# VectorE's products of three batches moved among the last row turns, and tile 0's routing put first in the adapter layer

## The chip, the cores and the metric

The kernel runs on one core of one Trainium2 chip. The metric is device time in microseconds (us) of one execution. PE is TensorE, DVE is VectorE, ACT is ScalarE, POOL is GpSimd, and SP issues the DMAs.

## The reference, cut to what matters

Four residual blocks follow each other, each on a layer norm of x, which is 4 batches x 512 rows x 1024 columns. Only the first two are touched by the change.

```
def _L0_attn_ref(x):            # for each of the 1024 columns l: attention among the 4 batches
    q = transpose(x, (2, 0, 1))                       # l, n, c
    scores = einsum('lnc,lmc->lnm', q, q) / scale     # 4 x 4 for each l
    prob = softmax(scores)
    return x + transpose(einsum('lnm,lmc->lnc', prob, q), (1, 2, 0))

def _L0_ffn_ref(x, W_base, b_base, W_gate, A, B):
    result = x @ W_base.T + b_base
    probs = softmax(x @ W_gate.T)                     # 8 experts
    top_p, top_i = top_k(probs, 2); top_p /= sum(top_p)
    h = einsum('bnd,erd->bner', x, A) * route_w[..., None]
    return result + einsum('bner,eor->bno', h, B) * SCALING
```

Then come an attention with 32 heads and a second adapter layer, which the change leaves alone. One of the weights of that attention, the query weights, is prepared while the first adapter layer runs.

## The kernel before, in words

Every stage is one block of five written-out instruction streams, one for each engine, tied by semaphores. A stage begins when all engines have ended the stage before. The rows are 16 tiles of 128.

**First layer (`first`, L601 to L1015).** Each tile t is normed: `dve_stats` on DVE, `pool_rstd` on POOL, and then the normalisation itself on the engine that the string `Norm.ON` (L60) names for it, "d" for DVE and "a" for ACT. Even tiles go to DVE, odd ones to ACT. The a-tiles also need `pool_shift`. PE turns (transposes) the normed tile in two halves (L706) and ACT copies both out of PSUM into `hT` (L774), where a row is one of the 1024 columns and a batch is 512 elements long. `hT` has 8 parts j. For each j, DVE makes the six products of different batches (`product`, L818 to L824, one instruction of 512 elements and its accumulator), ACT the four squares (`square`, L749), DVE the softmax of the 4 x 4 scores (`softmax`, L826), and then the weighted sums are made by ACT (`weigh`), DVE (`weigh_more`, L857) and, through 128 x 256 diagonals that POOL writes (L921), by PE (`messages`, L685). DVE adds the messages to x (L863). Products and squares of j=0 and j=1 stand ahead of the loop over j. Those of j+2 are dealt out among the four row tiles c of the loop by `fourth(c)`, which cuts the list `pairs` in four. All products wait for all 16 tiles. In between, `side` runs the making of fused weights: `absorbed(G)` with loads of `wuk` and `wqn`, products on PE (L667), copies on ACT (L733) into four staging tiles `mst`, and stores. `fused(kt)` does the same for the output weights (L677, L741, L742). A load of `absorbed(2)` is issued by SP behind the stores of `absorbed(0)`. At the end of the stage the first 8 of 14 parts of the adapter layer's weights are split into a high and a low half-precision part by ACT (L1177) and DVE (L1184), and PE makes the first column chunk of tiles 0 and 1.

**Adapter layer (`lora_layer0`, L1187 to L1512).** PE follows the list `ORDER` (L1212): ("c", t, c) is column chunk c of tile t (24 matmuls), ("w", t) turns the routed factors of tile t (L1260), ("a", t) is the adapter's product (6 matmuls), ("s", n) is a small total. DVE makes the routing (`gate`, L1352 to L1382, 13 short instructions with one exponential on ACT, L1295), adds the chunks to x (`finish`, L1392) and then the adapter's part (`adapter`, L1400). POOL makes the low half of each normed tile (L176) and adds the bias to x (`add_bias`, L1453), for which `finish` waits. A tile t+2 is normed, split (ACT L171, POOL L176) and turned by a DMA (L183) while tile t is worked on.

For t=5 to 13 the query weights (`QueryWeights`) go along, one group g a tile: DVE weighs them (L402, L403), ACT squares them (L408), PE totals (L412), DVE and POOL make the scale (L416, L419), ACT writes the high part (`act_high`, L430) and DVE the low part (`dve_low`, L435). ACT's high part stands last in the turn of a tile. DVE's low part stands ahead of `finish`.

Of the kernel before, what the change touches and what calls it, by code (L numbers as in the profile page):

```python
# [56 lines left out]
class Norm:  # L57


    ON = "da" * 8 + "d" * 19 + "a" * 13 + "d" * 16  # L60
# [136 lines left out]
def layers(nc, a, out):  # L197
    root = ExitStack()
    with root:
# [34 lines left out]
        with ExitStack() as right:  # L234
            with ExitStack() as both:
                g["room"] = right.enter_context(nc.sbuf_tensor("N_room", [128, 6144], F, side="right"))
                g["s_c"] = root.enter_context(nc.semaphore("F0_c"))

                g["bk"] = bk = [banks.enter_context(nc.psum_tensor(f"bk{i}", [128, 512], F)) for i in range(2)]
                feed.place_first(g["room"])  # L240
# [12 lines left out]
            projections(**g)  # L253
# [346 lines left out]
def first(nc, a, wbd, mwd, cst, vec, half, ident, xb, norm, msq, lnr, room, feed, lw, ones, s_c, bk, keep, **_):  # L600
# [3 lines left out]
    hb = [room[:, 5120:6144]] + [ph.sb(f"h{i}", [128, D]) for i in range(1, 3)]  # L604
# [35 lines left out]
    pairs = [(n, m) for n in range(4) for m in range(n, 4)]  # L640
    apart = [p for p in pairs if p[0] != p[1]]

# [82 lines left out]
    def act(e):  # L725
        w = Waits(e)

        def absorbed(G):
            for k in range(2):
                n = staged("a", G, k)  # L730
                w.wait_ge(s_wp, 2 * G + k + 1)
                w.wait_ge(s_mst[n % 4], 16 * (n // 4))
                e.activation(mst[n % 4][:, :], wb[k][:, :], ACT.Copy).then_inc(s_we, 1)  # L733
# [34 lines left out]
        for t in range(NT):  # L768
            if t + 2 < NT and t % 2:
# [45 lines left out]
    def dve(e):  # L815
        w = Waits(e)

        def product(j, n, m):  # L818
            k = 6 * j + apart.index((n, m))
            w.wait_ge(s_hT, 2 * NT)  # L820
            w.wait_ge(s_tr, 2 * NT)
            w.wait_ge(s_sc, k)
            e.tensor_tensor_reduce(junk, hT[:, j, 512 * n:512 * n + 512], hT[:, j, 512 * m:512 * m + 512], 1.0, 0.0, ALU.mult, ALU.add,
                                   sc[:, j, n, m:m + 1]).then_inc(s_sc, 1)  # L824

        def softmax(j):  # L826
            w.wait_ge(s_sc, 6 * j + 6)
# [42 lines left out]
        for t in range(NT):  # L870
# [3 lines left out]
            if t + 2 < NT and t % 2 == 0:  # L874
                w.wait_ge(s_tr, 2 * t)
                norm.dve_apply(e, w, t + 2, hb[(t + 2) % 3][:, :], xb[:, t + 2, :])
        for n, m in apart:
            product(0, n, m)
# [3 lines left out]
        for n, m in apart:  # L882
            product(1, n, m)
# [27 lines left out]
    def pool(e):  # L911
# [15 lines left out]
        for t in range(NT):  # L927
            if t + 2 < NT and t % 2:
# [11 lines left out]
        feed.pool_low(e, w, 1)  # L940

    def sp(e):
# [54 lines left out]
        for j in range(KD):  # L997
# [3 lines left out]
            for c in range(4):  # L1001
                side(SIDE_J.get((j, c)))
        for n in range(4):
# [183 lines left out]
def lora_layer0(nc, a, cst, vec, half, ident, ones, xb, xd, s_xd, lnr, norm, feed, lw, wa, qw, ms, s_c, bk, **_):  # L1187
# [3 lines left out]
    W, BT, bias = lw.W, lw.BT, ph.sb("bias", [128, D])  # L1191
# [9 lines left out]
    s_xb, s_g, s_gx = ph.sem("xb"), ph.sem("g"), ph.sem("gx")  # L1201
# [10 lines left out]
    ORDER = [("c", 0, 1), ("c", 1, 1), ("w", 0), ("c", 0, 2), ("w", 1), ("a", 0), ("c", 1, 2), ("a", 1)]  # L1212
    for t in range(2, NT):
# [69 lines left out]
    def act(e):  # L1283
# [13 lines left out]
        for n in range(8, 10):  # L1297
            lw.act_split(e, w, n)
        feed.act_high(e, w, 2)
        gate_exp(0)  # L1300
        for n in range(10, 12):
            lw.act_split(e, w, n)
        gate_exp(1)
        high_w(0)
# [4 lines left out]
        for t in range(2, NT):  # L1309
            gate_exp(t)  # L1310
# [11 lines left out]
            if QW < t <= QW + 8:  # L1322
                qw.act_high(e, w, t - QW - 1)

    def dve(e):
# [75 lines left out]

        stats(2)
        lw.dve_split(e, w, 8)
        apply(2)
        lw.dve_split(e, w, 9)
        gate(0)
# [6 lines left out]
        low_w(1)  # L1413
        stats(3)
        apply(3)
        stats(4)
        finish(0)
# [3 lines left out]
        for t in range(2, NT):  # L1421
            stats(t + 3)
# [6 lines left out]
            gate(t)  # L1429
# [17 lines left out]
    def pool(e):  # L1447
        w = Waits(e)

        def add_bias(t):  # L1450
            norm.applied(w, N_F0 + t)
            w.wait_ge(lw.s_bias, 16)
# [12 lines left out]
        add_bias(0)  # L1465
        feed.pool_low(e, w, 2)
        add_bias(1)
# [20 lines left out]
    def sp(e):  # L1488
# [7 lines left out]
        e.dma_start(bias[:, :], a["b0"].partition_broadcast(128)).then_inc(lw.s_bias, 16)  # L1496
# [1032 lines left out]
```

## Time and profile before

| what | value |
|---|---|
| median of 3 runs | 1631.84 us (1630.63 to 1632.85) |
| the profiled execution | 1631.13 us, span 1629.3 us |
| PE busy | 1547.9 us, 95% |
| DVE busy | 1018.8 us, 63% |
| ACT busy | 868.9 us, 53% |
| POOL busy | 811.3 us, 50% |
| the first layer | 0 to about 171 us of the span |
| the adapter layer | about 171 to 404 us of the span |

Busy shares are means over all stages. The two stages that the change touches are the first quarter of the span, and each has its own limits. A row of the timeline gives start, duration, engine, line and tile, and in brackets how long the engine stood idle before it and what released it. A row with "x2" merges two instructions.

### The profile page before, as it was taken

The page shows a single profiled execution, that of the slowest core. Times are in us where ns is not written, and L with a number is a line of the kernel's source. Part 1 is how long each engine was busy: PE and PEld are TensorE (multiplying, and loading weights), DVE is VectorE, ACT ScalarE, POOL GpSimd, SP SyncE. Part 2 cuts the span into 40 slices and gives each one's busy share as a digit, 9 for nine tenths or more (in the row PEclk, how much of TensorE's full clock was granted, in tenths as well). Part 3 has the DMA queues.
Part 4 walks back from the last instruction along what each step waited for, and adds up shares of the span by engine and source line. Part 5 has one row for each costly group of instructions (what it writes and reads, how often), then busy time and mean ns, then how long its engine had stood idle before and what let it go on. Part 6 is the DMA issues. An engine that isn't in the chain of part 4 may idle for free. (4 is left out here: it accounts for less than half of the span.)

```text
span 1629.3 us, 31927 instructions
## 1 busy us (share of the span) xinstructions
PE 1547.9 (95%) x12366; PEld 950.2 (58%) x12366; DVE 1018.8 (63%) x2747; ACT 868.9 (53%) x1654; POOL 811.3 (50%) x699
## 2 busy tenths in 40 slices
PE   5898899999989999999999999889999999999998
PEld 4655455555556776777777777644444444465554
DVE  7898857776778888888888888832110010344433
ACT  6886222221759999999999999931210000211110
POOL 4223244444957888888888888830010000244440
PEclk9999899999999999999999999999999999999999
DMA  9894334444756999999998999997763331233331
GB/s 359 297 330 149 91 88 107 143 142 128 154 120 112 187 173 189 179 184 187 195 190 174 184 185 173 178 208 226 176 167 80 101 91 26 75 66 84 83 86 65
DMA packets 560263, 249.82 MB, mean 153 GB/s; under 512 B 502256, under 2 KB 535152, under 8 KB 559984
## 3 DMA queue, kind: packets, MB, share of 16 engines
q1 hardware_dynamic: 560112, 247.78, 66.1%
q8 instruction: 98, 1.61, 0.4%
q14 instruction: 53, 0.43, 0.1%
HBM read 73.68 MB, written 48.23 MB: 75 GB/s over the span
## 5 line engine op out<-in xcount | busy, mean ns | idle before, releaser
L1967 POOL TENSOR_TENSOR xb<-xb 128x1280 f16<-128x1280 f32 x128 | 335.6, 2622 | 7.8 <-ACT xb L1870 7.8
L1862 ACT ACTIVATE xb<-bk,D_sv,qw_c 128x512 f32<-128x512 f32 (+3 forms) x512 | 289.3, 623 | 4.4 <-DVE D_sv L1925 4.2
L1916 DVE TENSOR_REDUCE bk<-bk 128x1 f32<-128x512 f32 (+3 forms) x512 | 228.3, 492 | 20.5 <-PE bk L1812 19.9
L92 POOL TENSOR_SCALAR mv<-mv 128x1 f32<-128x1 f32 x64 | 31.2, 488 | 279.1 <-DVE mv L87 278.1
L1870 ACT ACTIVATE xb<-xb 128x1280 f16<-128x1280 f32 x128 | 162.7, 1271 | 13.1 <-DMA xb<-xb 9.3
L1803 PE MATMUL bk<-kTh,D_QTh 128*128 128x512 f16 (+3 forms) x512 | 153.4, 300 | 6.3 <-ACT xb L1862 6.2
L1804 PE MATMUL bk<-kTl,D_QTh 128*128 128x512 f16 (+3 forms) x512 | 153.2, 299 | 0.0
L1805 PE MATMUL bk<-kTh,D_QTl 128*128 128x512 f16 (+3 forms) x512 | 146.5, 299 | 0.0
L1827 PE MATMUL D_t<-vh,xb 128*128 128x65 f16 x1280 | 131.5, 194 | 4.7 <-DMA xb<-xb 3.0
L1828 PE MATMUL D_t<-vl,xb 128*128 128x65 f16 x1280 | 131.6, 193 | 0.0
L1829 PE MATMUL D_t<-vh,xb 128*128 128x65 f16 x1280 | 131.0, 193 | 0.0
L1827 PEld LDWEIGHTS D_t<-vh,xb 128*128 128x128 f16 x1280 | 119.1, 97 | 5.3 <-DMA xb<-xb 3.2
L2086 DVE SCALAR_TENSOR_TENSOR xb<-bk,ms_c,xb 128x512 f32<-128x512 f32 x22 | 15.5, 747 | 167.0 <-PE bk L50 167.0
L1828 PEld LDWEIGHTS D_t<-vl,xb 128*128 128x128 f16 x1280 | 118.9, 98 | 0.4
L1829 PEld LDWEIGHTS D_t<-vh,xb 128*128 128x128 f16 x1280 | 119.1, 97 | 0.0
L1940 DVE TENSOR_TENSOR D_QTl<-D_t,D_QTh 128x512 f16<-128x512 f32 x128 | 88.6, 692 | 46.9 <-ACT D_QTh L1879 46.9
L2408 POOL TENSOR_TENSOR xb<-xb,F_bias 128x1024 f32<-128x1024 f32 x16 | 38.2, 2393 | 131.7 <-DMA F_mean<-in_cst 131.7
L1973 POOL TENSOR_TENSOR D_os<-D_on,D_os 128x256 f16<-128x256 f32 x128 | 87.5, 684 | 10.7 <-ACT D_os L1886 10.7
L527 POOL TENSOR_TENSOR D_qs<-D_qs,keep 128x256 f32<-128x256 f32 x84 | 61.0, 727 | 58.6 <-DVE keep L522 58.6
L171 ACT ACTIVATE N_hl<-N_h 128x1024 f16<-128x1024 f32 x26 | 27.4, 1054 | 107.4 <-DVE N_h L105 107.2
L50 PE MATMUL bk<-E_mh,ow_ot 128*128 128x512 f16 x220 | 83.4, 379 | 0.0
L48 PE MATMUL bk<-E_mh,ow_ot 128*128 128x512 f16 x220 | 83.4, 379 | 0.0
(331 smaller groups left out, 4383.9 us busy)
## 6 DMA issues: line engine op xcount, KB each, us to landing
od<-D_os SPq DMA_DIRECT2D x32, 512.0 KB, 4.5
xd<-xb SPq DMA_DIRECT2D x16, 512.0 KB, 4.2
ow_raw<-mwd SPq DMA_DIRECT2D x16, 512.0 KB, 4.7
xb<-xd SPq DMA_DIRECT2D x16, 512.0 KB, 5.9
out_x<-xb SPq DMA_DIRECT2D x16, 512.0 KB, 3.0
xb<-in_x SPq DMA_DIRECT2D x6, 1024.0 KB, 13.6
A_wo<-in_wo SPq DMA_DIRECT2D x6, 1024.0 KB, 7.5
ow_raw<-in_w SPq DMA_DIRECT2D x16, 384.0 KB, 4.3
```

Source lines behind the costliest of these rows:

```text
L1803: e.matmul(ps, qh, kT[0][:, k0:k0 + M], start=i > 0, stop=False)
L1804: e.matmul(ps, qh, kT[1][:, k0:k0 + M], start=False, stop=False)
L1805: e.matmul(ps, ql, kT[0][:, k0:k0 + M], start=False, stop=False)
L1827: e.matmul(o, pt[:, c, :], v[0][:, t, 0:65], start=j == 0, stop=False)
L1828: e.matmul(o, pt[:, c, :], v[1][:, t, 0:65], start=False, stop=False)
L1829: m = e.matmul(o, pt[:, 10 + c, :], v[0][:, t, 0:65], start=False, stop=j == i)
L1862: m = e.activation(p[:, AT[i]:AT[i] + N], Sb[n % 4][:, c:c + N], ACT.Exp, scale=qw.col(qw.NEG, g), bias=s[:, 7 - i:8 - i])
L1870: e.activation(P2[u % 3][:, 0:1280], P[u % 3][:, :], ACT.Copy).then_inc(s_ph, 1)
L1916: m = e.tensor_reduce(minima(u, i), Sb[n % 4][:, c:c + N], AX.X, ALU.min)
L1940: e.tensor_tensor(lo[:, :], t_bank("t", u)[:, :], hi[:, :], ALU.subtract).then_inc(s_tl, 1)
L1967: e.tensor_tensor(P2[u % 3][:, 1280:2560], P[u % 3][:, :], P2[u % 3][:, 0:1280], ALU.subtract).then_inc(s_pl, 1)
L1973: e.tensor_tensor(o[:, :, 1, 64 * h:64 * h + 64], on[u % 2][:, :, :], o[:, :, 0, 64 * h:64 * h + 64], ALU.subtract).then_inc(s_ol, 1)
```

## The change

Four edits stand in the diff.

1. First layer: tiles 14 and 15 are both normed by DVE. The six products of j=0 and j=1 that need only batches 0 to 2 wait for tiles 0 to 11 alone and run directly behind DVE's last norm. Their unused elementwise output goes to the staging tile `mst[3]`, so ACT's first use of it waits for them. The list `pairs` is in another order, so the third quarter of a loop has one product and the last has two.
2. The bias of the adapter layer gets its place in the first layer (it takes over the buffer of `hb[1]`), is loaded near the stage's end, and POOL adds it to tiles 0 and 1 in the first layer, not in the adapter layer.
3. Adapter layer: DVE begins with the routing of tile 0. The order of the parts, norms, `finish` and routing of tiles 0 to 2 is another on DVE and ACT, and PE's `ORDER` has the chunks of tile 2 between the adapters of tiles 0 and 1.
4. For t=6 to 13 ACT makes the query weights' high part first in its turn, not last.

```
-    ON = "da" * 8 + "d" * 19 + "a" * 13 + "d" * 16
+    ON = "da" * 7 + "d" * 21 + "a" * 13 + "d" * 16
...
-    hb = [room[:, 5120:6144]] + [ph.sb(f"h{i}", [128, D]) for i in range(1, 3)]
+    hb = [room[:, 5120:6144], bias, ph.sb("h2", [128, D])]
...
-    pairs = [(n, m) for n in range(4) for m in range(n, 4)]
+    pairs = [(n, m) for m in range(4) for n in range(m + 1)]
+    TIMES = [(j, p) for j in range(2) for p in apart[:3]] + [(j, p) for j in range(2) for p in apart[3:]]
+    TIMES += [(j, p) for j in range(2, KD) for p in apart]
...   act, absorbed
+                w.wait_ge(s_sc, 6 if n == 3 else 0)
...   dve, product
-            w.wait_ge(s_hT, 2 * NT)
-            w.wait_ge(s_tr, 2 * NT)
+            w.wait_ge(s_hT, 8 * m + 8)
...
+            if k >= 6:
+                w.wait_ge(s_tr, 2 * NT)
...   dve, after the last norm
-        for n, m in apart:
+        for j in range(2):
+            for n, m in apart[:3]:
+                product(j, n, m)
+        for n, m in apart[3:]:
             product(0, n, m)
         softmax(0)
...
-        for n, m in apart:
+        for n, m in apart[3:]:
             product(1, n, m)
...   pool, end of the first layer
+        for t in range(2):
+            norm.applied(w, N_F0 + t)
+            w.wait_ge(lw.s_bias, 16)
+            e.tensor_tensor(xb[:, row(t), :], xb[:, row(t), :], bias[:, :], ALU.add).then_inc(s_xb, 1)
...   sp, first layer, ahead of the turns
+        w.wait_ge(s_msg, 28)
+        e.dma_start(bias[:, :], a["b0"].partition_broadcast(128)).then_inc(lw.s_bias, 16)
...   adapter layer
-    ORDER = [("c", 0, 1), ("c", 1, 1), ("w", 0), ("c", 0, 2), ("w", 1), ("a", 0), ("c", 1, 2), ("a", 1)]
-    for t in range(2, NT):
+    ORDER = [("c", 0, 1), ("c", 1, 1), ("w", 0), ("c", 0, 2), ("w", 1), ("c", 1, 2), ("a", 0), ("c", 2, 0), ("a", 1), ("c", 2, 1),
+             ("w", 2), ("c", 2, 2), ("a", 2)]
+    for t in range(3, NT):
...   act
-        for n in range(8, 10):
+        lw.act_split(e, w, 8)
+        gate_exp(0)
+        for n in range(9, 12):
             lw.act_split(e, w, n)
         feed.act_high(e, w, 2)
-        gate_exp(0)
-        for n in range(10, 12):
-            lw.act_split(e, w, n)
+        high_w(0)
         gate_exp(1)
-        high_w(0)
...
         for t in range(2, NT):
+            if QW < t <= QW + 8:
+                qw.act_high(e, w, t - QW - 1)
             gate_exp(t)
...
-            if QW < t <= QW + 8:
-                qw.act_high(e, w, t - QW - 1)
...   dve
+        gate(0)
+        lw.dve_split(e, w, 8)
         stats(2)
-        lw.dve_split(e, w, 8)
+        lw.dve_split(e, w, 9)
         apply(2)
-        lw.dve_split(e, w, 9)
-        gate(0)
...
         low_w(1)
+        finish(0)
         stats(3)
         apply(3)
-        stats(4)
-        finish(0)
         adapter(0)
         finish(1)
         adapter(1)
         for t in range(2, NT):
+            if t == 2:
+                gate(t)
+                stats(t + 2)
             stats(t + 3)
             apply(t + 2)
...   pool, adapter layer
-        add_bias(0)
         feed.pool_low(e, w, 2)
-        add_bias(1)
```

## Rows read from the trace of the kernel before

**Rows 1.** Windows, one stretch: busy time (instructions) of PE, PEld, DVE, ACT, POOL, clock, DMA.
```profile
130.00:140.00 10.00, 8.46 (x40) 5.53 (x38) 9.21 (x25) 8.26 (x21) 2.09 (x3) 1.00 0.57 199
```

**Rows 2.** Timeline of all engines, the last row turns.
```profile
35.38 1.24 ACT L110 ACTIVATE N_room<-xb,mv 128x1024 f32<-128x1024 f32 x1 [0.33 <-POOL mv L100]
36.52 1.06 ACT L774 ACTIVATE F_room<-A_tr 128x512 f32<-128x512 f32 x2
...
39.57 0.69 DVE L823 CUSTOM_DVE_ANT_0 N_room<-F_room 128x512 f32<-128x512 f32 x1 [5.30 <-ACT F_room L774]
```

**Rows 3.** The same timeline, from the first store to the loop over j.
```profile
41.55 0.88 SPq L962 DMA_DIRECT2D wbd<-keep  x2
...
43.98 0.29 DVE L830 COPY A_sc<-A_sc 128x3 f32<-128x3 f32 x3
...
48.79 3.67 PE L667 MATMUL bk<-N_room 128*128 128x128 f32 x16 [3.23 <-DMA N_room<-in_wqn]
...
56.06 0.29 DVE L830 COPY A_sc<-A_sc 128x3 f32<-128x3 f32 x3 [0.17 <-ACT N_room L754]
...
61.13 1.41 DVE L857 SCALAR_TENSOR_TENSOR A_h<-F_room,A_ex,A_h 128x512 f32<-128x512 f32 x2 [2.07 <-ACT A_h L765]
```

**Rows 4.** Timeline, end of the first layer and start of the next.
```profile
158.55 4.79 DVE L1184 SCALAR_TENSOR_TENSOR F_room<-F_room,F_sc 128x784 f16<-128x784 f32 x3
159.81 2.70 POOL L176 TENSOR_TENSOR N_room<-N_room 128x1024 f16<-128x1024 f32 x1 [2.02 <-ACT N_room L171]
...
164.34 3.81 DVE L1184 SCALAR_TENSOR_TENSOR F_room<-F_room,F_sc 128x768 f16<-128x768 f32 x4 [0.67 <-ACT F_room L1177]
...
171.49 0.32 PE L48 MATMUL bk<-F_room,N_room 128*128 128x384 f16 x1 [0.48 <-PEq L1008]
```

**Rows 5.** Timeline, routing of tile 0.
```profile
176.84 2.36 POOL L1453 TENSOR_TENSOR xb<-xb,F_bias 128x1024 f32<-128x1024 f32 x1 [2.35 <-DMA F_bias<-in_b]
176.91 2.31 DVE L1365 CAST F_sm<-F_mi 128x2 f32<-128x2 uint32 x1
184.38 0.47 PE L1260 MATMUL F_tr<-cst,F_hw 128*128 128x128 f32 x1 [4.93 <-DVE F_hw L1381]
```

**Rows 6.** Timeline, tile 1's adapter, tile 2's routing, PE's turns of tiles 2 and 3.
```profile
198.46 0.39 PE L48 MATMUL F_tr<-F_room,F_hwh 128*128 128x512 f16 x1 [2.21 <-DVE xb L1400]
205.63 0.23 DVE L1358 TENSOR_SCALAR F_sm<-bk,F_sc 128x8 f32<-128x8 f32 x1 [1.56 <-PE bk L50]
207.84 0.29 DVE L1381 TENSOR_TENSOR F_hw<-bk,F_sm 128x128 f32<-128x128 f32 x1
209.33 0.27 PE L1260 MATMUL F_tr<-cst,F_hw 128*128 128x128 f32 x1
222.51 0.27 PE L1260 MATMUL F_tr<-cst,F_hw 128*128 128x128 f32 x1
```

**Rows 7.** Windows, the stretch behind tile 1's adapter.
```profile
198.50:202.50 4.00, 4.00 (x13) 1.70 (x14) 3.96 (x8) 0.00 (x0) 0.41 (x1) 0.57 0.71 131
```

**Rows 8.** Groups of DVE by form, 171 to 223 us: busy us, mean ns, idle before.
```profile
L1400 DVE SCALAR_TENSOR_TENSOR xb<-F_tr,F_sc,xb 128x512 f32<-128x512 f32 x6 | 4.2, 747 | 0.2
L83 DVE BATCH_NORM_STATS2 st<-xb 128x6 f32<-128x512 f32 x5 | 3.4, 687 | 3.2 <-PEq L1008 3.2
L1392 DVE SCALAR_TENSOR_TENSOR xb<-F_o,F_sc,xb 128x384 f32<-128x384 f32 x4 | 2.4, 612 | 0.4 <-PE F_o L50 0.4
```

**Rows 9.** Timeline, one step with query weights (t=10) and the next exponential.
```profile
325.18 2.35 POOL L1453 TENSOR_TENSOR xb<-xb,F_bias 128x1024 f32<-128x1024 f32 x1
327.44 1.28 DVE L435 SCALAR_TENSOR_TENSOR F_room<-F_room,qw_c 128x1024 f16<-128x1024 f32 x1 [1.52 <-ACT F_room L430]
331.01 0.38 PE L412 MATMUL F_tr<-qw_c,ones 128*128 128x1 f32 x2 [0.80 <-DVE xb L1400]
336.22 0.20 ACT L1295 ACTIVATE F_sm<-F_sm 128x1 f32<-128x1 f32 x1 [8.82 <-DVE F_sm L1363]
```

**Rows 10.** Waits, 240 to 372 us: who for whom, us in total, times, longest.
```profile
PE F_tr L412 <- DVE xb L1400: 8.6, 8, 1.6
```

More of the change, by code:

```diff
@@ L239, in layers @@
                 g["bk"] = bk = [banks.enter_context(nc.psum_tensor(f"bk{i}", [128, 512], F)) for i in range(2)]
+                g["bias"] = both.enter_context(nc.sbuf_tensor("F0_bias", [128, D], F))
+                g["s_xb"] = root.enter_context(nc.semaphore("F0_xb"))
                 feed.place_first(g["room"])
@@ L597, in pe_turned, with first @@
             w.wait_ge(self.s_o[j % 3], 16 * self.G * (1 if j % 3 else 2) + 16 * (j // 3))
-def first(nc, a, wbd, mwd, cst, vec, half, ident, xb, norm, msq, lnr, room, feed, lw, ones, s_c, bk, keep, **_):
+def first(nc, a, wbd, mwd, cst, vec, half, ident, xb, norm, msq, lnr, room, feed, lw, ones, s_c, bk, keep, bias, s_xb, **_):
     ph = Scope(nc, "A")
     hT = lw.room[:, :].rearrange("p (k n) -> p k n", k=KD)
-    hb = [room[:, 5120:6144]] + [ph.sb(f"h{i}", [128, D]) for i in range(1, 3)]
+    hb = [room[:, 5120:6144], bias, ph.sb("h2", [128, D])]
     tr = [ph.bank(f"tr{i}") for i in range(2)]
@@ L768, in act @@
         for t in range(NT):
-            if t + 2 < NT and t % 2:
+            if t + 2 < NT and norm.ON[t + 2] == "a":
                 w.wait_ge(s_tr, 2 * t)
@@ L818, in product @@
         def product(j, n, m):
-            k = 6 * j + apart.index((n, m))
-            w.wait_ge(s_hT, 2 * NT)
-            w.wait_ge(s_tr, 2 * NT)
+            k = TIMES.index((j, (n, m)))
+            w.wait_ge(s_hT, 8 * m + 8)
             w.wait_ge(s_sc, k)
-            e.tensor_tensor_reduce(junk, hT[:, j, 512 * n:512 * n + 512], hT[:, j, 512 * m:512 * m + 512], 1.0, 0.0, ALU.mult, ALU.add,
+            if k >= 6:
+                w.wait_ge(s_tr, 2 * NT)
+            e.tensor_tensor_reduce(junk if k >= 6 else mst[3][:, :], hT[:, j, 512 * n:512 * n + 512], hT[:, j, 512 * m:512 * m + 512], 1.0, 0.0, ALU.mult, ALU.add,
                                    sc[:, j, n, m:m + 1]).then_inc(s_sc, 1)
         def softmax(j):
-            w.wait_ge(s_sc, 6 * j + 6)
+            w.wait_ge(s_sc, 6 * j + 6 if j else 9)
             w.wait_ge(s_sq, 4 * j + 4)
@@ L873, in dve @@
                 norm.dve_stats(e, w, t + 3, xb[:, t + 3, :])
-            if t + 2 < NT and t % 2 == 0:
+            if t + 2 < NT and norm.ON[t + 2] == "d":
                 w.wait_ge(s_tr, 2 * t)
                 norm.dve_apply(e, w, t + 2, hb[(t + 2) % 3][:, :], xb[:, t + 2, :])
-        for n, m in apart:
+        for j in range(2):
+            for n, m in apart[:3]:
+                product(j, n, m)
+        for n, m in apart[3:]:
             product(0, n, m)
@@ L927, in pool @@
         for t in range(NT):
-            if t + 2 < NT and t % 2:
+            if t + 2 < NT and norm.ON[t + 2] == "a":
                 norm.pool_shift(e, w, t + 2)
@@ L1184, in dve_split, with lora_layer0 @@
         e.scalar_tensor_tensor(lo, self.source(self.again + n), self.scale(c), hi, ALU.mult, ALU.subtract).then_inc(self.s_wl, 1)
-def lora_layer0(nc, a, cst, vec, half, ident, ones, xb, xd, s_xd, lnr, norm, feed, lw, wa, qw, ms, s_c, bk, **_):
+def lora_layer0(nc, a, cst, vec, half, ident, ones, xb, xd, s_xd, lnr, norm, feed, lw, wa, qw, ms, s_c, bk, bias, s_xb, **_):
     ph = Scope(nc, "F0")
     qw.place(*[lw.room[:, o:o + 2048] for o in lw.free])
-    W, BT, bias = lw.W, lw.BT, ph.sb("bias", [128, D])
+    W, BT = lw.W, lw.BT
     junk = lw.room[:, lw.free[1] + 2048:lw.free[1] + 2560].bitcast(H16)
@@ L1200, in lora_layer0 @@
     s_tp, s_hi, s_tr = ph.sem("tp"), ph.sem("hi"), ph.sem("tr")
-    s_xb, s_g, s_gx = ph.sem("xb"), ph.sem("g"), ph.sem("gx")
+    s_g, s_gx = ph.sem("g"), ph.sem("gx")
     s_fin = ph.sem("fin")
@@ L1428, in dve @@
                 qw.dve_weigh(e, w, t - QW, vec, lnr, wa)
-            gate(t)
+            if t > 2:
+                gate(t)
             if t == NT - 1:
@@ L1451, in add_bias @@
             norm.applied(w, N_F0 + t)
-            w.wait_ge(lw.s_bias, 16)
             e.tensor_tensor(xb[:, row(t), :], xb[:, row(t), :], bias[:, :], ALU.add).then_inc(s_xb, 1)
@@ L1494, in store @@
             e.dma_start(xd[row(t), :, :], xb[:, row(t), :]).then_inc(s_xd, 16)
-        e.dma_start(bias[:, :], a["b0"].partition_broadcast(128)).then_inc(lw.s_bias, 16)
         wa.sp_load(e)
```

## The prediction

> **What bounds the kernel now.** I read the two stages of the change in five views. The windows [rows 1] say that in the loop over j of the first layer DVE is busy 9.21 of 10 us and PE 8.46: DVE sets the pace there, and a shift of its start is handed on. The timeline of the last row turns [rows 2] shows DVE idle for 5.30 us until 39.57, behind ACT: ACT norms tile 15 at 35.38 and then copies out three tiles one after the other, from 36.52 until it releases DVE at 39.57, about 1.0 a tile. ACT ends last there. The next view [rows 3] shows what follows. The stores of `absorbed(0)` leave at 41.55, the load behind them lets PE go at 48.79 after 3.23 us of waiting, ACT's squares of j=1 end just ahead of DVE's softmax at 56.06 (0.17 idle), and DVE waits 2.07 for ACT's first weighing of j=1 at 61.13. So the start of the loop hangs on ACT and on that load, not on DVE's products.
>
> In the adapter layer PE waits 4.93 us at 184.38 for the routing of tile 0 [rows 5], 2.21 us at 198.46 for tile 1's adapter [rows 6], and 8.6 us in eight totals of the query weights [rows 10]. The profiled execution took 1631.13 us for a span of 1629.3, 0.71 under the median, so a difference in the span is taken off the median.
>
> **Step 1, the last row turns.** Tile 15's norm leaves ACT. DVE can start it when the scale is there, about 35.1 (ACT's needs the shift besides, 0.3 more), and has it done at 35.9; PE turns the tile from about 36.0. ACT goes on with tile 13's copies at 34.95 instead of 36.52 (tile 12's pair ends then), and three tiles at the pace of before end at 37.95 instead of 39.53. Gain: 1.58 us in `hT` complete.
>
> The six early products take 0.73 each (0.69 and a step), 4.4 us, from 35.9 to 40.3. Three more of j=0 then end at 42.45. Without early products, six would begin at 37.98 and end at 42.4. So for softmax(0), now at 43.98 [rows 3], the early products buy nothing; it comes at 42.5 either way. For softmax(1) they take three products (2.2 us) off DVE ahead of 56.06. Before, DVE and ACT came out together there, and both move up 1.5, so DVE's extra 2.2 become idle time behind ACT. I cost them at 0, with up to 0.2 either way. ACT's new wait for six products (due 40.3) lies before the copy that has it (about 42.3).
>
> ACT, the stores at 41.55 and the load all move by 1.58, and the loop over j with them. Its DVE work is the same. The new order of pairs lets PE's transposes at c=0 start a product (0.7) earlier, but DVE's pace rules, so 0. Step 1: 1.6 us gained. Its lower end is 0, if the load does not come earlier; its upper 2.0.
>
> **Step 2, the bias on POOL in the first layer.** Before, two bias additions (2.36 each [rows 5]) and a low half ran on POOL beside tile 0's routing. Its CAST of two elements began at 176.91 and ended at 179.22, with POOL's addition (176.84 to 179.20). DVE stood still until POOL was through, and from there to PE's turn at 184.38 two more POOL instructions passed. The same shows at 158.55 [rows 4]: three splits took 4.79 in place of 2.9 while one POOL instruction ran from 159.81 to 162.51. An instruction of one engine waits for the other's end.
>
> The Trainium skill says this too (SBUF — State Buffer, section "Who interferes with whom"): DVE with two SBUF inputs or in a two-port mode and a GpSimd instruction exclude each other for a whole instruction, and the one that issues first wins. The rows above agree. What the rule speaks against is step 4.
>
> Now the additions follow POOL's low half of tile 1 at 162.5. They collide with DVE's five last splits, about 0.95 each [rows 4, 8]. In turns: the third split to 163.3, addition to 165.7, split 4 to 166.65, addition to 169.0, three splits to 171.9. Before, DVE ended at 168.15 and PE at 171.01, with the next stage's PE at 171.49 [rows 4]. So DVE now ends last and the stage ends 0.9 later. Bounds: 0 (if POOL's additions slip in between) and 2. The bias's load took under 5.6 us (stage start to 176.84 [rows 4, 5]) and is issued, behind the 28th message, some 15 us ahead of the additions. Cost: 0.9 us.
>
> **Step 3, order of tiles 0 to 2.** I write the new order down from the stage's start S. Durations: routing 2.5 (205.63 to 208.13), statistics 1.45, norm 0.75, split 0.95, `finish` 1.55, adapter 1.35 (its two instructions overlap) [rows 6, 8]. For PE, 13.18 a tile [rows 6] less 0.25 for the turn and 1.3 for six adapter matmuls gives 3.9 a chunk.
> - DVE: routing(0) to 2.7, split 8, statistics 2, split 9 to 6.1, norm 2 to 7.6, splits 10 and 11 to 9.5. Then routing(1) meets POOL's low half of tile 2 (9.5 to 11.65) and ends at 13.2.
> - PE: two chunks to 8.0, turn 0 at once (it waited 4.93), chunk (0,2) to 12.1, then 1.2 of waiting for routing(1), chunk (1,2) to 17.5, adapter 0, chunk (2,0) to 22.7, adapter 1, chunk (2,1), turn 2 at 28.0, chunk (2,2) to 32.1.
> - DVE meanwhile: `finish(0)` to 16.6, tile 3 to 19.75, adapter 0 to 21.1, `finish(1)`, adapter 1 to 24.9, routing(2) to 27.4, statistics 4 and 5 to 30.3, norm 4 to 31.05. ACT's high half comes first, so the low part of tile 2's factors is there at 32.8 and PE waits 0.7. POOL's low half and bias end at 36.7, `finish(2)` and adapter 2 at 39.65, tile 5's norm at 41.85, routing(3) at 44.35.
> - PE is through with (3,0) and (3,1) at 41.95 and waits 2.5. Turn 3 at 44.4.
>
> Before, turn 3 stood at 222.51, which is 51.2 behind the stage's start of about 171.3 [rows 4, 6]. So 6.8 are gained up to there. The adapter's `finish(3)` is then late behind the bias, and the totals after tile 3 lose 1.0 more. A wait of 2.21 was followed by a stretch at a granted clock of 0.57 [rows 7], mostly the lower level of 1.2 GHz, worth some 2 us of PE. The new wait of 2.5 may bring the same; as DVE is the later one there, I take half, 1.0. Step 3: 6.8 - 1.0 - 1.0 = 4.8 gained, with bounds 1 and 7.
>
> **Step 4, the query weights' high part first.** In one step [rows 9] DVE waits 1.52 for ACT's L430, makes the low part at 327.44 and `finish` behind it, and PE's total waits 0.80. With the high part made ahead of the routing's exponential, DVE could start 1.5 earlier, at 325.95. Taken alone, adapter t would be bound by PE from then on: 0.55 less of PE's wait of 0.80 in the steps like this one (four of them), about twice that in the three with longer waits (up to 1.6 [rows 10]), some 5.4 us in all. But POOL's bias addition runs from 325.18 to 327.53, and the low part has two SBUF inputs, like the splits that stood still at 158.55. It would then begin at 327.5, as now, and `finish` also waits for the addition. I take 0.1 a step, 0.3 to 0.5 in all. By the skill's rule just named it is 0 and by shared bandwidth some 3.
>
> **Sum.** 1.6 - 0.9 + 4.8 + 0.4 = 5.9 us. 1631.84 - 5.9 = 1625.9; I say 1626.
>
> **Rivals.**
> - A: step 4 pays in full, since the low part is not held up, and 5.4 come in place of 0.4: 1621. For it: eight waits that all name DVE [rows 10]. Against it: rows 4 and 5.
> - B: step 1 is lost, since the load sets PE's 48.79 and does not move: 1627.5. For it: PE did wait for that DMA. Against it: the load is issued behind the stores that wait for ACT, and PE's wait counts from that issue.
> - C: the new order of tiles 0 to 3 only puts the wait off. Two statistics stand ahead of norm 4, so bias 2, `finish(2)`, routing(3) stay late for two or three tiles, each with a spell at the lower clock. Step 3 is then worth 1 to 2: 1629.3.
> - D, slower: ACT's high part at the head of its turn waits for POOL's scale and holds up the exponential and the high half of tile t+2, so PE's turn waits. Now the exponential comes at 336.22, 5.2 behind the total at 331.01, after ACT has been idle for 8.82 [rows 9]; total and scale take about 1.3 of the 5.2. From a delay of over 4 us on, each of eight steps costs the excess, and with 2 us each it is 16 less the 6: 1642. It decides where the totals come late, which they don't in this trace.
> - E: the first edit doesn't bring the norm of tile 15 forward, because DVE's turn needs ACT's copies of the ring anyway; this is B's time again and held within it.
>
> **Chances.** Forecast 0.48, A 0.15, B with E 0.13, C 0.19, D 0.03, and 0.02 for something else. Faster by over 0.2% (below 1628.6, about what a measurement of this kernel can tell from no change): nearly all of the forecast, A and B, a third of C: 0.77. Within 0.2%: 0.18. Slower: 0.05. The range reaches from A's 1621 to a little above C: 1620.5 to 1630.
>
> **What would show it.** Step 1: ACT's last copy (L774) ends near 38 and DVE's loop starts near 59.6 instead of 61.13; the early products stand from 35.9. Step 2: POOL's two L1453 in the first layer, DVE's last split of the stage after PE's last chunk. Step 3: no wait at turn 0, a wait of 2 to 3 us at turn 3. Step 4: L435 starts on the end of POOL's addition, its duration over 2 us in place of 1.28, and PE's waits at L412 stay near 8 us. If L412's waits fall to 3 us, step 4 was judged wrong; if turn 3 waits 5 us or more, C.

## The result and the profile after

The kernel after takes 1622.44 us (median of 6 runs, 1620.99 to 1623.14), the kernel before 1631.78 us in the runs beside it (6 runs, 1630.33 to 1632.85). The ratio is 0.9941, with a 95% interval of 0.9931 to 0.9951: 9.3 us faster, where 5.9 were forecast. The time lies inside the range given, but 1622.44 is nearer to rival A's 1621 than to the forecast of 1626, so the number alone doesn't say which account was right. The traces do. The profiled execution took 1622.44 us for a span of 1620.7, so its span is 8.6 shorter than the span before.

The places that the prediction followed, in the two profiled executions (us from the start of the span; the forecast is the prediction's sum up to that place):

| place | before | after | moved | forecast |
|---|---|---|---|---|
| DVE's norm of tile 14 (no part of the change) | 33.49 | 32.36 | -1.1 | 0 |
| `hT` complete, ACT's first square | 39.56 | 36.87 | -2.7 | -1.6 |
| DVE's start of the loop over j | 61.13 | 57.77 | -3.4 | -1.6 |
| adapter layer, PE's first chunk | 171.49 | 168.60 | -2.9 | -0.7 |
| PE's turn of tile 3 | 222.51 | 212.29 | -10.2 | -7.5 |
| PE's turn of tile 4 | 237.27 | 227.64 | -9.6 | -5.5 |
| PE's first matmul of the next stage | 404.88 | 394.20 | -10.7 | -5.9 |
| end of the span | 1629.3 | 1620.7 | -8.6 | -5.9 |

The first line comes from the load of tile 1's x. DVE's statistics of that tile wait for it, and start at 6.12 in this execution against 7.43 before; of that, 1.1 us are left at tile 14's norm. In the traces of all kernels here this start lies anywhere between 6.12 and 8.00, so it is taken off before the first layer is read. At the other end, 2.1 of the 10.7 us were lost again behind the adapter layer, in code that is the same. The other kernels below ended between 0.9 us to the good (the one with the bias alone, 5.4 ahead at 399.45 and 6.3 at the end) and 1.4 to the bad there. So this is probably the one execution's and not the change's, which no run settles. It is why the parts are measured below inside their own stage.

First layer, timeline of the kernel after. Columns as in the rows ahead of the prediction: start us, duration us, engine, line, operation, tiles, shapes, and in brackets the idle time before it and who ended it.
```profile
33.95 0.81 DVE L105 TENSOR_SCALAR N_room<-xb,mv 128x1024 f32<-128x1024 f32 x1 [0.82 <-POOL mv L95]
34.68 0.68 DVE L831 CUSTOM_DVE_ANT_0 A_mst<-F_room 128x512 f32<-128x512 f32 x1
...
35.70 1.14 ACT L781 ACTIVATE F_room<-A_tr 128x512 f32<-128x512 f32 x2
36.87 0.63 ACT L761 ACTIVATE N_room<-F_room 128x512 f32<-128x512 f32 x1
...
38.86 0.88 SPq L977 DMA_DIRECT2D wbd<-keep  x2
...
46.06 3.04 PE L673 MATMUL bk<-N_room 128*128 128x128 f32 x16 [3.19 <-DMA N_room<-in_wqn]
...
52.71 0.29 DVE L838 COPY A_sc<-A_sc 128x3 f32<-128x3 f32 x3 [1.52 <-ACT N_room L761]
...
57.77 1.41 DVE L865 SCALAR_TENSOR_TENSOR A_h<-F_room,A_ex,A_h 128x512 f32<-128x512 f32 x2 [1.53 <-ACT A_h L772]
```
The norm of tile 15 now stands on DVE, the products directly behind it, and ACT's last copy ends at 36.8. Everything that hung on ACT in [rows 2, 3] has moved with it: the first store by 2.69, PE's wait for the load by 2.73 (its length is the same, 3.23 and 3.19). Most of what the early products saved turned into idle time: DVE waits 1.52 for ACT ahead of its second softmax, where it waited 0.17 [rows 3].

End of the first layer and routing of tiles 0 and 1, same kernel and view:
```profile
156.16 2.70 POOL L176 TENSOR_TENSOR N_room<-N_room 128x1024 f16<-128x1024 f32 x1 [2.02 <-ACT N_room L171]
158.82 6.10 POOL L955 TENSOR_TENSOR xb<-xb,F_bias 128x1024 f32<-128x1024 f32 x2
...
160.69 6.90 DVE L1201 SCALAR_TENSOR_TENSOR F_room<-F_room,F_sc 128x768 f16<-128x768 f32 x4 [0.67 <-ACT F_room L1194]
...
168.60 0.32 PE L48 MATMUL bk<-F_room,N_room 128*128 128x384 f16 x1 [0.48 <-PEq L1025]
...
176.40 0.27 PE L1278 MATMUL F_tr<-cst,F_hw 128*128 128x128 f32 x1
...
178.24 1.47 DVE L1380 TENSOR_TENSOR F_sm<-F_sm 128x1 f32<-128x1 f32 x1
...
181.50 0.33 PE L1278 MATMUL F_tr<-cst,F_hw 128*128 128x128 f32 x1 [0.94 <-DVE F_hw L1398]
```
The two additions and the last four splits wait for each other: 6.10 us for what takes 4.7, and 6.90 in place of the 3.81 of [rows 4]. In return there is no wait at PE's turn of tile 0, which was 4.93 [rows 5].

The turn of tile 2 and what follows, same kernel and view:
```profile
202.35 2.35 POOL L1472 TENSOR_TENSOR xb<-xb,F_bias 128x1024 f32<-128x1024 f32 x1
204.73 1.01 DVE L1409 SCALAR_TENSOR_TENSOR xb<-bk,F_sc,xb 128x256 f32<-128x256 f32 x2 [4.06 <-POOL xb L1472]
...
212.29 0.33 PE L1278 MATMUL F_tr<-cst,F_hw 128*128 128x128 f32 x1 [2.22 <-DVE F_hw L1398]
...
218.62 1.05 PE L328 MATMUL F_tr<-wa_c,ones 128*128 128x1 f32 x8 [0.80 <-DVE xb L1417]
```
The wait was put off: `finish(2)` stands 4.06 us for POOL's addition, and PE 2.22 at tile 3's turn, behind it. No drop of the clock followed this time (windows of the kernel after, columns as in [rows 1]):
```profile
212.50:216.50 4.00, 4.00 (x26) 2.41 (x25) 0.55 (x2) 0.28 (x1) 3.71 (x2) 1.00 0.70 70
```
In four us 26 matmuls ran at a granted clock of 1.00, where [rows 7] had 13 at 0.57.

One step with query weights (t=9, as t=10 in [rows 9]), timeline, then the waits of PE from 228 to 362 us:
```profile
307.61 1.15 ACT L433 ACTIVATE F_room<-F_room,qw_c 128x1024 f16<-128x1024 f32 x1 [5.85 <-POOL qw_c L422]
...
314.40 0.27 PE L1278 MATMUL F_tr<-cst,F_hw 128*128 128x128 f32 x1
...
314.82 2.35 POOL L1472 TENSOR_TENSOR xb<-xb,F_bias 128x1024 f32<-128x1024 f32 x1
...
315.48 2.77 DVE L438 SCALAR_TENSOR_TENSOR F_room<-F_room,qw_c 128x1024 f16<-128x1024 f32 x1
```
```profile
PE F_tr L415 <- DVE xb L1417: 7.5, 8, 1.3
```
ACT's high part is there nearly 7 us early and DVE starts its low part without waiting for it, but the low part lasts 2.77 in place of 1.28 and ends at 318.2, 1.1 behind the end of POOL's addition (317.2).

### The profile page after: what moved, and what is told of

Its sections match the earlier page's. It is cut to its first block and busy times, and to the rows that moved or that the text cites. A ratio compares the mean times of both kernels' runs of the same rounds, so it can differ in the third digit from the quotient of the medians.

```text
span 1620.7 us, 31929 instructions
## 1 busy us (share of the span) xinstructions
PE 1546.0 (95%) x12366; PEld 949.4 (59%) x12366; DVE 1028.4 (63%) x2748; ACT 868.4 (54%) x1653; POOL 813.1 (50%) x698
## 5 line engine op out<-in xcount | busy, mean ns | idle before, releaser
L48 PE MATMUL bk<-E_mh,ow_ot 128*128 128x512 f16 x220 | 83.4, 379 | 0.0
L49 PE MATMUL bk<-E_ml,ow_ot 128*128 128x512 f16 x220 | 83.4, 379 | 0.0
```

What stands on the lines that cost most here:

```text
L48: e.matmul(out, a[0], b[0], start=start, stop=False, **kw)
L49: e.matmul(out, a[0], b[1], start=False, stop=False, **kw)
```

## The experiments

Each time is a median of 5 to 12 executions. Each ratio, with its 95% interval, is to the kernel before on the same chip, whose medians there were 1631.4 to 1631.6 us. The kernels were timed in four groups on four chips: the first four; then e_bias, e_order, b_ahead and b_both; then m_old, b_old and b_lean; then e_later. Across groups the ratios compare better than the medians.

**The bare first edit, e_norm15.** Kernel before, with tile 15's norm moved to DVE:
```
-    ON = "da" * 8 + "d" * 19 + "a" * 13 + "d" * 16
+    ON = "da" * 7 + "d" * 21 + "a" * 13 + "d" * 16
-            if t + 2 < NT and t % 2:
+            if t + 2 < NT and norm.ON[t + 2] == "a":
```


> The kernel before with tile 15 normed by VectorE and nothing else changed. If the gain of the first layer comes from taking that norm off ScalarE: hT is complete 1.6 us sooner (VectorE's first product near 38.0 by the span of before, against 39.57), the loop over j starts about 2 us sooner, and the time falls by 1.5 to 2.5 us. If the early products are what pays: no more than 0.5 us.

Measured: 1629.91 us, ratio 0.9993 (0.9984 to 1.0002). The time alone can't tell it from nothing. Its trace can. From the norm of tile 14 to `hT` complete it was 6.07 us before and is 4.51 here (33.93 to 38.44), 1.56 less against 1.58 forecast. From that norm to the loop over j it was 27.64 and is 25.94, 1.7 less.

**The early products alone, e_products.** The new order of pairs, the six early products and ACT's wait for them, without the norm:
```
+        for j in range(2):
+            for n, m in apart[:3]:
+                product(j, n, m)
+        for n, m in apart[3:]:
             product(0, n, m)
...
```


> The kernel before with the six early products and the new order of pairs; tile 15 stays with ScalarE. If the products buy nothing by themselves: hT complete as before, the softmax of j=0 about 2.2 us sooner (three products less behind it), but the squares of j=0 and j=1 on ScalarE and the load behind the first stores keep their places, so VectorE only waits longer for ScalarE, and the time moves by less than 0.5 us. If VectorE's products set the start of the loop: 1.5 to 2 us less time.

Measured: 1631.3 us, ratio 1.0 (0.9991 to 1.0009). DVE's timeline of this kernel:
```profile
56.95 0.29 DVE L834 COPY A_sc<-A_sc 128x3 f32<-128x3 f32 x3 [2.96 <-ACT N_room L757]
```
DVE has 2.2 us of products less to do here and waits 2.96 for ACT instead of 0.17. ACT's squares set this point, as the prediction had it. One part of the expectation missed: `hT` is complete 6.58 us behind tile 14's norm, not 6.07. The early products run on DVE from 34.45, beside POOL's two short instructions for the scale and shift of tile 15. These take 0.86 and 0.46 there instead of 0.56 and 0.26, and ACT's norm of the tile waits for them. With the norm on DVE ahead of the products (e_first, the kernel after) this doesn't occur.

**The whole first edit, e_first.** Both together.

> The kernel before with the whole first edit (tile 15's norm and the early products) and nothing else. If the two only add up as the steps say: as with tile 15's norm alone, within 0.5 us of it, 1.5 to 2.5 us under the kernel before. If the pair is worth more than its parts, since the products would otherwise end behind ScalarE's squares once the norm has moved: at least 1 us under the run with the norm alone.

Measured: 1629.08 us, ratio 0.9986 (0.9977 to 0.9995), a gain of 0.8 to 3.8 us. From tile 14's norm to the loop it is 26.26 us, 0.3 more than with the norm alone. In this execution the 16 matmuls behind the load took 3.78 us at a granted clock of 0.50, against 2.69 at 0.73 with the norm alone; that alone is more than the 0.3. So the two traces don't show that the products are worth nothing. With the norm alone, DVE's six products of j=1 run without a pause until 54.7, ACT's squares are done at 53.9, and ACT then waits 1.67 for DVE where it waits 0.84 here. In that execution the early products would have saved up to 0.8 us.

**The fourth edit alone, e_high.** Kernel before, ACT's high part ahead of the exponential:
```
         for t in range(2, NT):
+            if QW < t <= QW + 8:
+                qw.act_high(e, w, t - QW - 1)
             gate_exp(t)
```


> The kernel before with ScalarE's high part of the query weights first in its turn, and nothing else. If VectorE's low part then waits for POOL's bias addition (one excludes the other): L435 takes about 2.8 us in place of 1.28 and ends where the addition ends plus 1.1, TensorE's eight waits at L412 fall from 8.6 to between 7 and 8 us in all, and the time falls by 0.5 to 1.2 us. If the two engines share the port by parts: L435 takes under 2 us, the waits fall to 3 to 5 us and the time falls by 3 to 5 us.

Measured: 1630.6 us, ratio 0.9996 (0.9987 to 1.0006). Its timeline and its waits, 228 to 362 us:
```profile
325.64 2.78 DVE L435 SCALAR_TENSOR_TENSOR F_room<-F_room,qw_c 128x1024 f16<-128x1024 f32 x1
...
330.71 0.38 PE L412 MATMUL F_tr<-qw_c,ones 128*128 128x1 f32 x2 [0.69 <-DVE xb L1400]
```
```profile
PE F_tr L412 <- DVE xb L1400: 7.6, 8, 1.3
```
The totals' waits fall from 8.6 [rows 10] to 7.6, and this agrees with the kernel after (7.5). The low part is held up by POOL's addition here too; rival A is out.

**The bias alone, e_bias.** Kernel before with the second edit: the bias row loaded in the first layer and POOL's additions for tiles 0 and 1 made there. The order of tiles 0 to 2 is the old one.
```
         feed.pool_low(e, w, 1)
+        for t in range(2):
+            norm.applied(w, N_F0 + t)
+            w.wait_ge(lw.s_bias, 16)
+            e.tensor_tensor(xb[:, row(t), :], xb[:, row(t), :], bias[:, :], ALU.add).then_inc(s_xb, 1)
...
-        add_bias(0)
         feed.pool_low(e, w, 2)
-        add_bias(1)
```


> The kernel before with only the bias moved: loaded and added to tiles 0 and 1 by POOL at the end of the first layer. The additions exclude VectorE's splits there, so the stage ends 0.8 us later; in the adapter layer the routing of tile 0 no longer meets them, only POOL's low half of tile 2. If those additions were what held the routing of tile 0: TensorE's wait of 4.93 us at the turn of tile 0 falls to about 1, and the time falls by 2 to 3.5 us net. If VectorE's order (statistics, splits and norm ahead of the routing) was the cause: the wait stays above 3 us and the time is within 1 us of before.

Measured: 1623.95 us, ratio 0.9957 (0.9943 to 0.9971), 7.6 us faster. The first timeline is of this kernel; PE's first chunk in it is at 172.84.
```profile
181.79 0.33 PE L1268 MATMUL F_tr<-cst,F_hw 128*128 128x128 f32 x1 [0.99 <-DVE F_hw L1389]
...
187.67 0.38 PE L48 MATMUL F_tr<-F_room,F_hwh 128*128 128x512 f16 x1 [1.28 <-DVE F_room L1192]
...
194.71 0.39 PE L48 MATMUL F_tr<-F_room,F_hwh 128*128 128x512 f16 x1 [1.68 <-DVE xb L1408]
...
217.09 0.27 PE L1268 MATMUL F_tr<-cst,F_hw 128*128 128x128 f32 x1
```
The wait at tile 0's turn falls from 4.93 to 0.99 with DVE's old order. Tile 3's turn comes 44.25 us behind the first chunk and tile 4's 59.0, against 65.78 before and 59.04 in the kernel after. So this edit alone gives the whole gain of the adapter layer's first four tiles.

The gain is more than twice the 2 to 3.5 us that I had expected, and the clock is the reason. Windows from the first chunk to tile 4's turn, and of four us behind tile 0's turn; first the kernel before, then this one:
```profile
171.49:237.27 65.78, 58.33 (x327) 33.17 (x328) 47.05 (x124) 15.12 (x28) 27.20 (x23) 0.92 0.32 81
184.38:188.38 4.00, 4.00 (x13) 2.01 (x14) 3.67 (x15) 1.50 (x4) 0.00 (x0) 0.50 0.18 33
```
```profile
172.84:231.84 59.00, 54.74 (x327) 31.84 (x327) 42.74 (x124) 15.13 (x28) 22.58 (x21) 1.00 0.33 81
181.79:185.79 4.00, 4.00 (x25) 2.40 (x25) 3.67 (x15) 1.58 (x5) 0.00 (x0) 1.00 0.56 102
```
Of the 6.8 us, 3.2 are shorter waits (7.41 in all before, 4.22 here). The other 3.6 are PE's own time: the same 327 matmuls take 58.33 us at a mean clock of 0.92 before, and 54.74 at 1.00 here. Before, the clock fell behind both long waits, 4.93 and 2.21. Here the waits are 0.99, 1.28 and 1.68, and it never fell.

**Bias and order, e_order.** The same with the third edit (the new `ORDER`, routing ahead of statistics, `finish(0)` before tile 3).

> The kernel before with the bias moved and the new order of tiles 0 to 2 (edits 2 and 3). By the written-out order: turn of tile 0 without a wait, a wait of 2.2 to 2.5 us at the turn of tile 3, and that turn 43.8 to 44.4 us behind the stage's start in place of 51.2; the time falls by 5.5 to 7 us less what the later stages take back, so 4.5 to 6. If most of this comes from moving the bias alone, it lies within 1.5 us of the run with only the bias moved.

Measured: 1625.17 us, ratio 0.9966 (0.9952 to 0.9979). The order adds nothing on top of the bias: tile 3's turn is 43.70 behind the first chunk (0.5 earlier than with the bias alone), tile 4's 60.19. The 1.2 us by which this is later than in the kernel after are the clock: it fell behind a wait of 2.22, and behind the same wait in the kernel after it didn't (timeline, then windows of this kernel):
```profile
215.97 0.33 PE L1269 MATMUL F_tr<-cst,F_hw 128*128 128x128 f32 x1 [2.22 <-DVE F_hw L1389]
```
```profile
216.00:220.00 4.00, 4.00 (x15) 2.06 (x16) 0.37 (x2) 0.28 (x1) 3.88 (x2) 0.57 0.33 62
```

**All but the order, m_old.** The kernel after without the third edit:
```
-    ORDER = [..., ("c", 1, 2), ("a", 0), ("c", 2, 0), ("a", 1), ("c", 2, 1), ("w", 2), ("c", 2, 2), ("a", 2)]
+    ORDER = [("c", 0, 1), ("c", 1, 1), ("w", 0), ("c", 0, 2), ("w", 1), ("a", 0), ("c", 1, 2), ("a", 1)]
-        gate(0)
+        stats(2)
         lw.dve_split(e, w, 8)
-        stats(2)
+        apply(2)
         lw.dve_split(e, w, 9)
-        apply(2)
+        gate(0)
...
```


> Edits 1, 2 and 4 with the old order of tiles 0 to 2 (the kernel after without edit 3). Theory (taking POOL's two additions out of the stage's head is what pays, the order adds nothing): 1621.2 us, between 1620.2 and 1622.6, so ratio about 0.9935 to the kernel before and a little under the kernel after; no wait of PE at turn 0 over 1.1 us, turn 4 about 59 us behind the stage's first instruction, as in the run with the bias alone. Rival (the order is worth the 4.8 us that the prediction gave it): 1627 us, turn 4 at 64.

Measured: 1621.87 us, ratio 0.9943 (0.9929 to 0.9956). That is the kernel after's 0.9941, and tile 4's turn is 59.00 behind the first chunk, again as in it. The third edit is worth nothing that can be told in the kernel after, neither for nor against.

**The additions moved within the stage, e_later.** Kernel before, one edit:
```
-        add_bias(0)
         feed.pool_low(e, w, 2)
-        add_bias(1)
         norm.pool_rstd(e, w, N_F0 + 3)
         feed.pool_low(e, w, 3)
+        add_bias(0)
+        add_bias(1)
```


> The kernel before with POOL's additions of the bias row for tiles 0 and 1 put behind its low parts of tiles 2 and 3, instead of ahead of them; nothing else changed. Theory (the additions cost their time where they meet VectorE's splits and routing of the stage's first 10 us): PE's wait at turn 0 falls from 4.93 us to about 1, as in the run with the bias moved to the first layer; the additions (2.36 us each) would then start near 23 us behind the stage's first instruction, where that run has VectorE's finish(0) some 19.5 us behind it, so finish(0) waits 4 to 5 us for them, and of the 7.6 us some 3 are left: 1628.5 us, 1627 to 1630. Rival (the additions cost what they take wherever they are in this stage): 1631.5 us, nothing gained. Rival (their waits are hidden there, moving them within the stage is as good as moving them out): 1624 us.

Measured: 1631.65 us, ratio 1.0005 (0.9997 to 1.0014). The time is that of the first rival, the mechanism that of the theory. The timeline of this kernel (its first chunk at 171.93):
```profile
180.89 0.33 PE L1260 MATMUL F_tr<-cst,F_hw 128*128 128x128 f32 x1 [1.00 <-DVE F_hw L1381]
...
193.37 4.64 POOL L1453 TENSOR_TENSOR xb<-xb,F_bias 128x1024 f32<-128x1024 f32 x2
195.74 1.01 DVE L1392 SCALAR_TENSOR_TENSOR xb<-bk,F_sc,xb 128x256 f32<-128x256 f32 x2 [4.18 <-POOL xb L1453]
...
198.12 0.61 PE L48 MATMUL F_tr<-F_room,F_hwh 128*128 128x512 f16 x1 [6.00 <-DVE xb L1400]
```
The wait at tile 0's turn fell to 1.00, as expected, so the additions beside the routing were what caused it. But `finish(0)` then waited 4.18 for them and PE 6.00 at tile 1's adapter, where it was 2.21 [rows 6]. My expectation left 3 us of gain, and all of it was paid back. Out of the stage, the same additions cost 0.8 us.

**One tile ahead, b_ahead.** The kernel after, with POOL making tile t+1's addition where it made tile t's:
```
+        add_bias(2)
         norm.pool_rstd(e, w, N_F0 + 4)
...
-                add_bias(t)
+                add_bias(t + 1)
```


> The changed kernel with POOL adding each tile's bias one tile ahead (tile 2's behind the low half of tile 3, tile t+1's behind the low half of tile t+2), so that no finish waits for it. The wait of 4.06 us of VectorE ahead of finish of tile 2 goes, and with it TensorE's 2.2 us at the turn of tile 3: 2 to 3 us less time. The low part of the query weights still meets a POOL addition of the same length at the same place, so if exclusion is what holds TensorE's totals, their waits stay at 0.68 to 1.33 each. If it was the wait for the bias that held them, they fall to 0.3 and the time falls by 5 us or more.

Measured: 1618.26 us, ratio 0.9926 (0.9913 to 0.994). The median is 4.2 below that of the kernel after, which was timed in another group. By the ratios (0.9941 there) it is 2.4, and the two intervals overlap a little. Timeline:
```profile
202.19 1.00 DVE L1409 SCALAR_TENSOR_TENSOR xb<-bk,F_sc,xb 128x256 f32<-128x256 f32 x2
...
203.95 2.35 POOL L1472 TENSOR_TENSOR xb<-xb,F_bias 128x1024 f32<-128x1024 f32 x1
```
`finish(2)` no longer waits, PE doesn't wait at tile 3's turn (211.51, 41.33 behind its first chunk at 170.18), and tile 4's turn is 56.09 behind it instead of 59.04.

**The same on the old order, b_old.** m_old with that addition ahead.

> The same with POOL's addition of the bias row one tile ahead of PE from tile 2 on. Theory (the 4 us that this gave on top of the kernel after came from POOL's order at every tile, whatever the order of tiles 0 to 2): 1617.2 us, between 1616 and 1618.5, under the 1618.3 that it gave with the new order. Rival (it only took back the waits that the new order of tile 2 had made, 4.06 us of VectorE ahead of finish(2) and 2.22 us of PE at turn 3, which the old order has not): the same as the run without it, 1621 us.

Measured: 1623.06 us, ratio 0.9946 (0.9933 to 0.996). No gain over m_old, and tile 4's turn stays 59.00 behind the first chunk: the rival was right. The addition ahead takes away a wait that only the new order has. Together the two give 2.9 us in the trace. On top of the moved bias, neither gives anything by itself.

**Without the early products, b_lean.** b_old without them.

> The same without the early products and the new order of pairs; tile 15's norm stays on VectorE. Theory (tile 15's norm on VectorE is all that pays in the first layer; in the profiled runs the diagonal blocks' loop started 25.94 us behind tile 14's norm with it alone, 26.26 with the products too): same as with them, within 0.5 us. Rival (the early products give what the prediction's range allowed them above zero, or the 0.8 us by which the medians of these two kernels alone differed): 0.8 us slower.

Measured: 1621.12 us, ratio 0.9939 (0.9926 to 0.9953), beside 0.9946 (0.9933 to 0.996) with them. The early products are worth nothing that these runs can tell; the intervals would hide the 0.8 us of e_norm15's trace.

**The low part late, b_both.** b_ahead, with DVE's weighing (L405, L406) behind the routing and the low part behind the total:
```
             if t > 2:
                 gate(t)
+            if QW <= t < QW + 8:
+                qw.dve_weigh(e, w, t - QW, vec, lnr, wa)
...
-                qw.dve_low(e, w, t - QW - 1)
...
+            if QW < t <= QW + 8:
+                qw.dve_low(e, w, t - QW - 1)
```


> As the run before it, and VectorE's low part of the query weights moved behind the adapter and the total of its tile, the weighing behind the routing. Now nothing long stands between the low part of the routed factors and finish. If exclusion by POOL's addition was what kept the eight waits at the totals: they fall to about 0.25 each, 5 us less than the changed kernel in these steps, and with the 2 to 3 us at tile 3 the time is 6 to 8 us under the changed kernel. If the totals wait for something else (adapter's place behind TensorE's own product): no more than the run before it.

Measured: 1621.6 us, ratio 0.9946 (0.9932 to 0.9959); my expectation missed. Timeline of this kernel, which shows the cause:
```profile
297.68 2.03 DVE L405 SCALAR_TENSOR_TENSOR F_room<-F_room,vec,lnr 128x256 f32<-128x256 f32 x1
299.40 2.53 POOL L1473 TENSOR_TENSOR xb<-xb,F_bias 128x1024 f32<-128x1024 f32 x1
299.64 2.44 DVE L406 TENSOR_SCALAR F_room<-F_room,vec,wa_c 128x256 f32<-128x256 f32 x1
```
The weighing's pieces, 0.48 and 0.41 us long in b_ahead, now met POOL's low half and its addition and took 2.03 and 2.44. The low part itself is free again (1.27 at 306.13), but seven of the eight totals still wait 1.03, since `finish` stands behind the weighing. I had moved one instruction out of the collision and two others into it.

## Why the prediction was right, and where not

**Step 1 held.** The norm gave 1.56 us in `hT` complete, in e_norm15 and in the kernel after once the earlier load is taken off; 1.58 were forecast. The early products gave nothing that the times can tell, as costed, and mostly for the reason given (DVE's idle 1.52 and 2.96 ahead of the second softmax). That holds while the matmuls behind the load are slow. In e_norm15, where they were faster, DVE's products came last, and the early ones would have been worth up to 0.8. By the loop over j it is 2.2 in the kernel after. The rest, 0.63, is that the 16 matmuls behind the load took 3.04 instead of 3.67 [rows 3], and ACT's copies and squares follow them. The granted clock was 0.64 in that stretch and 0.53 before; over the traces here it lay between 0.50 and 1.00. So the 0.6 is the execution's luck. Rivals B and E are out: the load moved with the stores.

**Step 2 has the right cost and the wrong account.** The stage's end was to come 0.9 later. From PE's first chunk at tile 0's low half (160.78 before, 157.14 after) to the next stage's first chunk it came 0.75 later. DVE did end last, by turns with POOL, as worked out. But step 2 was booked as a cost only. What the two additions had cost in the adapter layer went to step 3's account.

**Step 3 is the step that failed, as a statement on its cause.** Its timeline of the new order came out well: turn 3 at 43.7 behind the first chunk (the forecast's 44.4 from the stage's start is 44.2 from there), a wait of 0.94 at turn 1 (1.2), one of 2.22 at turn 3 (2.5). But 6.8 us were called the gain of the order, and e_bias shows that moving the bias gives them without it: with the old order, turn 3 stands at 44.25. The prediction named the mechanism itself, that DVE stood still beside POOL's additions [rows 5]. It didn't write down the old order without them. That would have shown a stage just as fast, since the 4.93 us at tile 0's turn shrink to 0.99 by themselves. What no run shows is the new order with the additions left in the stage. The routing of tile 0 would run ahead of them there, so the order might have had part of the gain by itself; shown is that it adds nothing once the bias has moved.

The second thing that the prediction lacked is what the clock gave back. It charged 1.0 for a fall of the clock behind the new wait, and looked at [rows 7] for that. It didn't look behind the 4.93 us, where the clock stood at 0.50. With 3.9 us a chunk it wrote the new order at the full clock and compared it with a trace that held two such falls. So its 6.8 contained some 3.6 us of clock without a word on them, and the agreement at turn 3 is in part luck: it holds because no long wait was left ahead of that turn.

**Step 3's size.** From the first chunk to tile 4's turn the gain is 6.74 (65.78 to 59.04), against 4.8. Of the miss of 1.9, 1.0 is the clock term: nothing was lost behind the wait of 2.22. In e_order the same wait was followed by 0.57 and cost 1.2. So the kernel after's execution fell on the good side, and one execution of each is too little to judge the weight of a half. The totals behind tile 3 lost 0.6 instead of 1.0, and turn 3 was 0.5 better. The distance itself isn't sharp: five kernels with the same code in this stretch (before, e_norm15, e_products, e_first, e_high) show 64.62 to 66.19.

Rival C had the right observation, that the wait is put off: `finish(2)` does stand for bias 2. But it is put off once, by 2.22 us, and not for two or three tiles.

**Step 4's mechanism held, and its size was put too small.** The low part met POOL's addition in every step and took 3.43 us in the first three and 2.77 in the other five. Against PE's turn it ends 0.12 us earlier than before (3.85 behind it, 3.97 in [rows 9] with the turn at 324.75), which is the 0.1 a step of the forecast. The eight steps together gave 1.05 against 0.4, since the two totals with the longest waits (1.62) fell to 1.33. Rival A, which had these waits gone, is out, though its time was the nearest. The Trainium skill's rule in SBUF — State Buffer, "Who interferes with whom", was set against this edit in the prediction. The trace agrees: an instruction on DVE of 1.28 us with two SBUF inputs took 2.77 or 3.43 beside POOL's of 2.35, in all eight steps.

**The sum.** Within the stages that were changed the kernel after gained 10.7, of which 1.1 is a load that landed early. That leaves 9.6 against 5.9: 1.9 from step 3, 0.65 from step 4, 0.6 from PE's faster matmuls behind the load, the rest spread over the first layer's terms. The runs' 9.3 us are close to that, but one trace isn't a median, and at least 1.6 of the 3.7 us of miss (the clock behind the 2.22 us and behind the load) are luck.

**What is open.** Why a wait of the same length is followed by a lower clock in one execution and not in another was not settled. The third edit without the second was not run. Of the 4.2 us between the medians of b_ahead and the kernel after, the traces show 2.9 up to tile 4's turn and 0.5 in the totals (7.0 against 7.5); the rest is within the intervals.

## What to carry to other kernels

When several edits touch one stretch, write the timeline once for each subset, above all with the old order and only the disturbing work gone. Here one edit gave all of the 6.8 us of the adapter layer's first four tiles, and the elaborate one beside it gave nothing until the work that it now waited for was pulled ahead too. When a long wait of PE goes, read the granted clock behind it as well: here it gave back as much as the wait. Before an instruction is moved on DVE, list what POOL runs at its new place. Moving work out of one collision paid only where it cost less at its new place: POOL's additions cost 0.8 us at the end of the first layer, but took back the whole gain when they only stood later in the stage.

## What the runs showed of the hardware that was not expected

- Small DVE instructions were held much as large ones are: one of 1 element a partition took 1.47 us beside POOL's L176 (the kernel after, 178.24), one of 2 elements 2.31 [rows 5], where the free ones take 0.14 and 0.17. Reading from PSUM with a small SBUF operand went on: L1398 (`bk,F_sm`) took 0.29 at 211.94 while POOL's L176 ran from 211.76 to 213.91.
- When both engines had work queued, they alternated and each paid: two additions and four splits took 6.10 and 6.90 us side by side, against 4.7 and 3.8 apart.
- Behind waits of PE of 4.93 and 2.21 us the granted clock was 0.50 and 0.57 for four us each (the kernel before). With waits of 0.99, 1.28 and 1.68 in their place it stayed at 1.00 (e_bias).
- A matmul stretch behind a wait of 2 to 3 us ran at a clock of 0.57 for some 3 us in one execution and at 1.00 in another of nearly the same code (wait 2.22 us in both). One profiled run can't answer a question of 0.2% by its span. The distance from a landmark inside the stage is better, but it still varied by 1.6 us among five kernels with the same code there.
